# Three rotating batch buffers without copies, two expert tiles split between transpositions, and a new order from rank to gate in a two-layer post-norm kernel

## The reference, cut to what matters

```python
x = ln(x + attn0(x))      # Gram matrix form of a normalised attention: x + gamma * weight_value
x = ln(x + ffn0(x))       # gate = softmax(x @ gate_w + gate_b), kept where >= 0.1, renormalised;
                          # out = sum over 8 experts of weight_e * (x @ expert_w[e] + expert_b[e])
x = ln(x + attn1(x))      # 16 heads of width 16; each token attends over its own 16 heads
x = ln(x + ffn1(x))       # scores = x @ w_router; the 768 best of 1024 tokens of a batch become
                          # gelu(x @ w_block), the others stay as they are
```

## Time and profile before

| | |
|---|---|
| median of 3 runs | 1359.78 us (1359.39 to 1360.84) |
| the profiled execution | 1357.91 us, span from first to last instruction 1356.1 us |
| PE busy | 1167.6 us, 86% of the span |
| DVE busy | 939.6 us, 69% |
| ACT busy | 723.5 us, 53% |
| POOL busy | 575.4 us, 42% |
| mean granted TensorE clock | 0.886 of full speed |

### The profile page before, as it was taken

The page is one execution under the profiler, slowest core; times in us unless marked ns, Lnnn a source line. Parts: engine busy times, 40 slices in busy tenths (PEclk is TensorE's granted clock), DMA queues, the critical chain, the costliest instruction groups (busy, mean ns, idle before and its releaser), DMA issues.

```text
span 1356.1 us, 31150 instructions
## 1 busy us (share of the span) xinstructions
PE 1167.6 (86%) x12264; PEld 749.5 (55%) x12264; DVE 939.6 (69%) x2118; ACT 723.5 (53%) x1152; POOL 575.4 (42%) x880
## 2 busy tenths in 40 slices
PE   6688899998989899998999989998999888996643
PEld 4444456655665546655665646555566555653532
DVE  3544578676766868677775868668776877656854
ACT  3223375347753575547853576447853566544444
POOL 2235335435354356345354355245354254350333
PEclk8789898799979997899979999799988998698566
DMA  5000092204802084202902065201902066108221
GB/s 187 16 1 16 31 154 21 80 9 113 114 3 78 19 173 44 79 9 92 135 2 79 17 164 56 56 24 61 170 6 64 1 138 81 38 27 156 33 79 47
DMA packets 93145, 90.64 MB, mean 67 GB/s; under 512 B 7110, under 2 KB 81864, under 8 KB 92744
## 3 DMA queue, kind: packets, MB, share of 16 engines
q1 hardware_dynamic: 80648, 75.54, 29.7%
q0 software_dynamic: 2560, 8.39, 1.8%
q10 hardware_dynamic: 9792, 4.72, 1.5%
HBM read 46.68 MB, written 41.94 MB: 65 GB/s over the span
## 4 chain that ended last, share of the span: by engine, by line
PE 55%; DVE 18%; DMA 6%; ACT 6%; issue 6%; POOL 6%; SPq 1%; ACTq 1%; POOLq 0%; DVEq 0%
PE bank L1852 52%; DVE keys L1546 2%; POOL rs L604 2%; DMA bt<-scratch_o 2%; DVE x L1435 2%; DVE stats L1294 2%; DVE gelu L1548 2%; DMA scratch_o<-stage 2%; PE bank L1862 2%; ACT x L915 1%; DVE ct L1263 1%; DVE gt L1349 1%; DVE x L1575 1%; ACT part L794 1%; ACT stage L794 1%
## 5 line engine op out<-in xcount | busy, mean ns | idle before, releaser
L1852 PE MATMUL bank<-we,at 128*128 128x512 f16 x1536 | 370.9, 400 | 1.9 <-DVE x L1435 1.9
L1852 PEld LDWEIGHTS bank<-we,at 128*128 128x128 f16 x1536 | 153.9, 102 | 192.4 <-issue 38.4
L619 POOL TENSOR_TENSOR part<-part 128x512 f32<-128x512 f32 x64 | 84.2, 1315 | 272.6 <-ACTq L941 272.6
L794 ACT ACTIVATE part<-bank,wexp 128x256 f32<-128x256 f32 x256 | 104.7, 472 | 160.3 <-PE bank L1852 99.7
L1435 DVE SCALAR_TENSOR_TENSOR x<-bank,wexp,x 128x256 f32<-128x256 f32 x256 | 122.7, 479 | 53.2 <-PE bank L1852 46.7
L1852 PE MATMUL bank<-bt,wqkv 128*128 128x512 f16 x576 | 137.1, 380 | 18.3 <-DVE stage L1263 12.3
L915 ACT ACTIVATE x<-x,nm,rs 128x256 f32<-128x256 f32 x192 | 104.5, 593 | 81.5 <-POOL nm L607 80.2
L1263 DVE TENSOR_TENSOR stage<-bank,stage 128x512 f16<-128x512 f32 x112 | 75.7, 686 | 86.5 <-ACT stage L794 86.2
L600 POOL TENSOR_SCALAR nm<-mv 128x2 f32<-128x2 f32 x128 | 33.6, 262 | 219.6 <-DVE mv L1299 213.9
L1852 PE MATMUL bank<-keys,blockdiag 128*128 128x16 f16 x3072 | 97.2, 193 | 22.1 <-DMA keys<-scratch_qkv 11.9
L1852 PEld LDWEIGHTS bank<-keys,blockdiag 128*128 128x128 f16 x3072 | 95.8, 103 | 26.9 <-issue 12.9
(11 more groups left out here) (197 smaller groups left out, 2239.6 us busy)
## 6 DMA issues: line engine op xcount, KB each, us to landing
scratch_qkv<-stage SPq DMA_DIRECT2D x40, 512.0 KB, 3.5
ct<-scratch_qkv SPq DMA_DIRECT2D x112, 128.0 KB, 6.8
x_in<-in_x_dram SPq DMA_DIRECT2D x32, 256.0 KB, 2.8
keys<-scratch_qkv SPq DMA_DIRECT2D x64, 128.0 KB, 6.1
bt<-scratch_o SPq DMA_DIRECT2D x16, 512.0 KB, 4.1
out_dram<-x POOLq DMA_DIRECT2D x32, 256.0 KB, 2.6
scratch_qkv<-part SPq DMA_DIRECT2D x8, 512.0 KB, 8.1
scratch_o<-stage SPq DMA_DIRECT2D x32, 128.0 KB, 3.5
```

What stands on the lines that cost most here:

```text
L619: pool.tensor_tensor(part[:, 0:2, :], part[:, 0:2, :], part[:, 2:4, :], ALU.add)\
L794: return act.activation(dst, src, ACT.Copy, scale=scale)
L1852: ins = pe.matmul(dst, lhs, rhs, start=(n == 0), stop=(n == len(terms) - 1))
```

## The change

- `x_in`, `x1` and `x3` go; `xb` is a list of three buffers, and batch n lives in `x_of(n) = xb[n % 3]` from loading to storing. The four `b_copy` of a batch and their semaphore go, and with them two waits of `a_apn`.
- A batch a >= 3 is loaded into the buffer that batch a - 3 leaves, so `load_x` waits also for `out_stored[p]` of batch a - 3. For batches 3 to 7 it moves on SP: pairs 0 and 1 behind the store of F7, pair 2 behind that of F9, pair 3 behind that of F11.
- PE: quarter 0 of expert tile 6 goes between `b_tz(c, 1)` and `b_tz(c, 2)`; quarter 3 of expert tile 3 goes between `b_pt(c, 2)` and `b_pt(c, 3)`, where DVE also puts two of its four v spreads between its reads of the two banks.
- From rank to gate: on DVE `a_ln2(b, 3)` stands ahead of the low half of c (now `a_cb_lo`), POOL's `ln(b, 7)` ahead of `ln(c, 4)`, and `b_ff`, `b_res`, `b_ffn`, `b_tx`, `a_apn` and `b_f` are interleaved in a new way on PE, ACT and DVE.

```diff
-        x_in = sb("x_in", [P, T, D])
+        xb = [sb(f"xb{i}", [P, T, D]) for i in range(3)]
...
-        x1 = sb("x1", [P, T, D])
-        x2 = x1
-        x3 = sb("x3", [P, T, D])
...
+        def x_of(b):
+
+            return xb[b % 3]
...
+                if a >= 3:
+                    sp.wait_ge(out_stored[p], 16 * (a - 2))
+                    sp.sem_inc(waits_held, 1)
+                sp.dma_start(x_of(a)[:, 2 * p:2 * p + 2, :], x_d[a][:, 2 * p:2 * p + 2, :])\
...
-                if a is not None:
+                if c is None:
                     for p in range(TP):
                         load_x(a, p)
...
                     b_loadq(b)
                     b_f(b, 7)
+                    if more:
+                        load_x(a, 0)
+                        load_x(a, 1)
                     b_f(b, 9)
+                    if more:
+                        load_x(a, 2)
                     b_f(b, 11)
+                    if more:
+                        load_x(a, 3)
                     b_loadk(b)
                     b_loadv(b)
...
-            def b_copy(b, p):
...
-                pool.tensor_copy(x3[:, 2 * p:2 * p + 2, :], x2[:, 2 * p:2 * p + 2, :])\
-                    .then_inc(x3_copied, 1)
...
-                if later(a):
-                    act.wait_ge(b_full, b_filled(a - 1, f"TX{p}"))
-                    act.wait_ge(x3_copied, 4 * (a - 1) + p + 1)
...
                 b_pt(c, 2)
+                b_spreadv(c, 1, range(2, 4))
                 b_pt(c, 3)
-                b_spreadv(c, 1, range(2, 6), last=True)
+                b_spreadv(c, 1, range(4, 6), last=True)
...
-                    a_moe(b, 3)
+                    a_moe(b, 3, (0, 1, 2))
                 if c is not None:
                     b_pt(c, 2)
+                if b is not None:
+                    a_moe(b, 3, (3,))
+                if c is not None:
                     b_pt(c, 3)
...
+                if b is not None:
+                    a_moe(b, 6, (0,))
+                if c is not None:
                     b_tz(c, 2)
```

More of the change, by code:

```diff
@@ L551, in turn @@
                 elif b is not None:
+                    more = a is not None and c is not None
                     b_f(b, 1)
@@ L955, in b_res @@
                 for t in range(2):
-                    ins = copy(x3_of(b)[:, 2 * p + t, :], x3_of(b)[:, 2 * p + t, :], mres[:, 2 * p + t:2 * p + t + 1])
+                    ins = copy(x_of(b)[:, 2 * p + t, :], x_of(b)[:, 2 * p + t, :], mres[:, 2 * p + t:2 * p + t + 1])
                 ins.then_inc(x3_scaled, 1)
             def b_ffn(b, p):
-                rows = [x3_of(b)[:, 2 * p + t, :] for t in range(2)]
+                rows = [x_of(b)[:, 2 * p + t, :] for t in range(2)]
                 act.wait_ge(b_rs, 8 * b + 4 + p + 1)
@@ L1093, in turn @@
                 if b is not None:
-                    b_tx(b, 2)
-                    a_ln2n(b, 3)
+                    b_f(b, 0)
+                if c is not None:
+                    b_ff(c, 2)
+                    b_res(c, 3)
+                if b is not None:
+                    b_f(b, 1)
                 if c is not None:
@@ L1098, in turn @@
                 if b is not None:
-                    b_tx(b, 3)
-                if c is not None:
-                    b_ff(c, 2)
+                    b_f(b, 2)
+                if a is not None:
+                    a_apn(a, 0)
                 if b is not None:
-                    b_f(b, 0)
-                    b_f(b, 1)
+                    b_f(b, 3)
                 if c is not None:
@@ L1683, in turn @@
                 if b is not None:
+                    a_ln2(b, 3)
+                if a is not None:
+                    a_cb_lo(a)
+                if b is not None:
                     b_tx(b, 0)
@@ L1686, in turn @@
                     b_ff(c, 0)
-                if b is not None:
-                    a_ln2(b, 3)
                 if a is not None:
                     a_tx(a, 3)
-                if c is not None:
-                    b_ff(c, 1)
                 if b is not None:
@@ L1698, in turn @@
                     b_tx(b, 2)
+                    b_tx(b, 3)
+                if c is not None:
+                    b_ff(c, 1)
                 if a is not None:
```

97 lines of the change are left out of this document (39 added, 58 removed).

## The result

The changed kernel takes **1375.01 us** (median of four runs, 1372.12 to 1388.44), against 1359.59 for four runs of the kernel before on the same chip. The ratio is 1.0135, 95% interval 1.0089 to 1.0181: slower by over 0.2%. Forecast were 1369, within 1350 to 1379. The sum came out near for the wrong reasons: one term was too small, one had the wrong size and, measured by itself, the wrong sign, and one that pays was put at nothing. The four runs lie 16 us apart, so the 15.4 us between the two kernels are known to about 6.

What follows compares the result with a forecast made beforehand. PE bounds nearly everywhere, turns of about 155 us, at most 4.2 us a turn to gain. Loads +10 and order -1 on the profiled 1357.91 gave 1366.9; the runs' median being 1.87 higher, 1368.8, said as 1369; range 1350 to 1379.

Steps and rivals of the forecast that it cites:

- late loads of x: Turns 2 to 6: loads held behind those of q on SP's queue, 2.0 us a turn, five turns, +10.
- order: New order from rank to gate: 0.5 us gained a turn, kept only in turns 1 and 7, -1.
- quarters: Quarter 0 of tile 6, at best 1.3 us a turn, and quarter 3 of tile 3: both put at 0.
- copies: 28 POOL copies of 0.61 us removed: 0 beyond the order's 0.5, bounds 0 and 0.6 us a turn.
- the wait for x takes it away again: Turns 2 to 6: the order's 0.5 us is lost, since the DMAs set the end there.
- Rival 2: ACT's or POOL's queueing before F5 costs 1 us a turn and all DMAs follow: +17, 1377; chance 0.15.
- Rival 3: Loads of x are not held behind those of q: 1358, no change; chance 0.16.
- the idle times that the forecast named: ACT idle before its third and fourth `xs` copy, waiting for a DMA from `in_x_dram`, five times some 3 us.
- second gate: Pair 3 lands late, `b_turnq` on ACT starts 4.5 us late, v comes 3.0 later: 0.6 to 2.1 a turn.
- walk: Instruction-by-instruction timing from rank to gate: F0 earlier, `a_apn(a, 1)` at 791.6 against 791.51, 0 to 0.6 us gained.
- What comes next waits for DVE, 94% busy: Behind tile 6's quarter 0, DVE's ranking from 745 to 769 holds PE, so the gain is 0.
- `out_stored`: `load_x` waiting for it costs nothing: `b_store` of pair 3 comes near 795, ahead of 801.0.

Runs made afterwards that it cites:

- 4: Changed kernel with its late loads of x issued by ACT on its own DMA queue behind the copy of F6: 1359.39 us.
- 3: Changed kernel with the old order from rank to gate; three buffers, late loads and quarters stay: 1376.58 us.
- 5: Changed kernel with loads of x issued by ACT on its own queue and the old order from rank to gate: 1349.96 us.
- 1: Kernel before with only SP's four loads of x moved late, as in the changed kernel: 1383.95 us.
- 2: Kernel before with only the new order from rank to gate; copies, early loads and whole tiles stay: 1366.67 us.
- 8: As 5, with tiles 3 and 6 whole again, leaving three buffers without copies: 1359.04 us.
- 10: Kernel before with only quarter 0 of expert tile 6 between `b_tz(c, 1)` and `b_tz(c, 2)`: 1345.92 us.
- 11: Kernel before with only quarter 3 of expert tile 3 between `b_pt(c, 2)` and `b_pt(c, 3)`, and DVE's two v spreads between its bank reads: 1357.98 us.
- experiment 9: Changed kernel with ACT's `a_wt` ahead of all four splits of x, no longer behind the first three: 1372.77 us.
- experiment 7: Changed kernel with all four loads of x on SP's queue directly ahead of the loads of q: 1358.97 us.

## Why the forecast was right, and where it was wrong

**The sum.** In medians, beside the forecast's terms (the profiles' span splits the same way in the table above):

| term | forecast | measured | from |
|---|---|---|---|
| late loads of x | +10 | +15.6 in the new order, +26.6 and +25.8 in the old one | after - 4; 3 - 5; 1 |
| order | -1 | +9.4 and +8.5 with x in time, -1.6 beside late loads | 4 - 5; 2; after - 3 |
| quarters | 0 | -9.1 (tile 6 alone -11.1, tile 3 +0.9) | 5 - 8; 10, 11 |
| copies | 0 | 0 to +2, not told from 0 | 8 |

The sign, the mechanism of the largest term and the range were right. That the median came within 6 us is luck: by the first entry of each row, errors of 6, 10 and 9 us partly cancel. The split between loads and order depends on which is taken out of the changed kernel first. If it is the order, the order costs nothing (-1.6), as the forecast said of turns 2 to 6 ("the wait for x takes it away again"), and the loads cost 26.6; then the loads are wrong by 17 us and the quarters by 9. A difference of two medians here is known to 4 to 6 us.

Rival 2 (the order loses too) is half right. The order does lose by itself, and the loads of q are issued 30.7 to 31.3 us behind rank, where experiment 3 with the old order has 30.2 to 30.8. But its 1377 adds this to the cost of the late loads, and experiment 3 shows that the two do not add; that it lies nearer to 1375 than the forecast does is luck as well. Rival 3 is refuted by the landings below.

**Late loads, mechanism right, size short.** The rule that what stands behind the loads of q waits for them held. In turn 5 pair 2 landed 152.6 us behind the start of the turn, forecast 150.8, and pair 3 at 155.7, forecast 152.9. It was not the late issue alone: pair 2 was issued at 144.3, and with the 2.8 us of the earlier trace rows it would have been there at 147.1, when ACT's third split began at about 147.8 in the kernel before. The transfers ahead of them ran a little slower than the rows before had it: the loads of q at 109 GB/s (804.8 to 812.2 us), where I had read 140. So ACT's rows:

```profile
819.86 0.63 ACT L784 ACTIVATE xs<-xb 128x512 f16<-128x512 f32 x1 [2.56 <-DMA xb<-in_x_dram]
820.39 0.26 ACT L784 ACTIVATE w16t<-bank 128x128 f16<-128x128 f32 x1
822.94 0.63 ACT L784 ACTIVATE xs<-xb 128x512 f16<-128x512 f32 x1 [2.29 <-DMA xb<-in_x_dram]
```

These are the idle times that the forecast named. `a_bias` comes 1.2 to 2.6 us later a turn, 9 us in five turns, about the forecast's 10. What it lacked is the clock behind that wait: in turns 2 and 5 (PE idle for 2.25 and 2.43 us, against 1.0 to 1.5 in the others) the 5 us up to the next turn became 6.5, 3.1 us in all. The other 3.5 of the 15.6 us I can't place; they are within the error of the medians. The step that failed outright is the second gate. I followed pair 3 to `b_turnq` and v. In turn 5 v was issued 163.7 us behind the start of the turn instead of 156.5, more than the forecast's 4.5 later, but the next turn began 5.3 us later too. POOL's wait for v got shorter (49.8 us), and PE's waits for POOL's `b_s` stayed at three (10.5 us, before 9.3). The reader that matters is the next Gram matrix, which experiment 9 lays bare.

**Order, walk right, clock left out.** The walk had `a_apn(a, 1)` unmoved behind `b_ffn(c, 2)`, and it was, within 0.8 us; F0 came 1.9 us earlier from rank (forecast 3), and gained nothing, as walked. But it gathered scattered idling into one stand of 2.24 us just ahead of work that runs without waits, and I priced a wait only by its length. F6 was not on time: from rank it ended 1.9 us late, although F5 had ended 2.3 us early.

**Quarters, the failed step.** "What comes next waits for DVE, 94% busy": that was an average over a window. The row on which it turns is PE's arrival at `b_rank`, without idling and 1.15 us behind its operand. The forecast had bounded the gain at 1.3 us a turn, which is what the stretch up to rank gained; I took the wrong end. That it "only moves the wait" was true of 0.6 of the 1.3 us, which PE waits ahead of `a_ap` instead. Turn 1, where the quarter shortens a wait of 4.22 us, and the clock that goes with it, it did not foresee.

**Copies, `out_stored`, tile 3's quarter:** nothing, as forecast. But in experiment 2, where copies and new order are together, ACT waited 2.85 us for POOL's copy before `a_apn(a, 0)` in turn 5. That the copies cost little holds in the kernel before, not in every order.

## What to carry to other kernels

Before an edit ahead of a meeting of two engines is priced at nothing, look at who arrives last there: a row without idle time means that its own engine is the bound, whatever the busy share of the other. When waits are rearranged, look at the longest one and at what follows it, and not at their sum alone: here a stand of 2.2 us on TensorE, with the clock behind it, cost 1.5 to 2.1 us more in four turns of six, where work without waits came next. Terms that share a stage do not simply add: take each out in both surroundings before you give it a price. A load that has 36 us of lead should not be put behind a queue's small-piece transfers; when it must go late, put it ahead of them (16 us here), and follow its data to every reader, the first one of the next stage too.

## What the runs showed of the hardware

- In one execution PE was granted a clock of 1.00 from rank to gate in two turns of six and 0.96 in four, although in two with and two without a drop the waits ahead of it are the same (0.98, 1.42, 2.23 us); of these, a turn with the drop was 1.4 to 2.1 us longer. In the changed kernel all six turns show 0.96. A drop behind waits of at most 1.5 us (experiments 3 and 8) cost 0.3 us, since PE waited less afterwards.
- Four loads of 256 KB landed after 3.8 us in the median ahead of the loads of q (experiment 7), and after 7.7 us behind them (the changed kernel), on the same queue; beside them, on ACT's queue, after 8.2 (experiment 4).
- The loads of q, in pieces of 512 bytes, moved 109 GB/s in the changed kernel, with the DMA engines' share at 1.25 (140 at 1.23 in the kernel before), and the stores and loads of x behind them up to 410 GB/s.
